# The next tile's loads issued in another order, in a recommender kernel on one core

## What is computed

```
e  = stack of tbl_f[ids[:, f]], f = 0..31        # [1024, 32, 16], called x0
xk = x0
for W in (W0, W1, W2):                            # W: [32, H, 64]
    xk = relu(einsum('bmd,bhd,mhk->bkd', x0, xk, W))
    outs.append(sum of xk over d)                 # 64 numbers per sample and layer
h  = concat(outs, dense_ctx)                      # 208 features
y  = relu(relu(h @ W_top1 + b1) @ W_top2 + b2) @ W_top3
```

## Time and profile before

| | |
|---|---|
| timed runs, median (lowest, highest) | 689.96 us (688.97, 692.24) |
| profiled execution, first to last instruction | 769.5 us |
| granted TensorE clock, mean | 0.918 |
| PE busy | 609.3 us, 79% |
| DVE busy | 577.9 us, 75% |
| POOL busy | 469.8 us, 61% |
| ACT busy | 236.9 us, 31% |
| DMA, all queues | 149.77 MB, mean 195 GB/s |

### The profile page before, as it was taken

The page is one execution under the profiler, slowest core; times in us unless marked ns, Lnnn a source line. Parts: engine busy times, 40 slices in busy tenths (PEclk is TensorE's granted clock), DMA queues, the critical chain, the costliest instruction groups (busy, mean ns, idle before and its releaser), DMA issues.

```text
span 769.5 us, 8172 instructions
## 1 busy us (share of the span) xinstructions
PE 609.3 (79%) x2818; PEld 219.3 (28%) x2818; DVE 577.9 (75%) x292; ACT 236.9 (31%) x440; POOL 469.8 (61%) x362
## 2 busy tenths in 40 slices
PE   0265179949996699939996499996997399999998
PEld 0121023313331134303332133322332133333334
DVE  0003199949994699849995599985995499999994
ACT  0022144206331154306431063425331063325331
POOL 6757447845797168853897258945897248704630
PEclk9978579979998699969999699998999599999999
DMA  5059800699039940699019950499329950399300
GB/s 169 7 154 373 306 1 1 226 356 366 21 124 327 363 153 4 193 393 361 19 41 333 377 214 5 146 342 373 104 56 337 358 215 6 105 376 372 105 1 0
DMA packets 58834, 149.77 MB, mean 195 GB/s; under 512 B 10728, under 2 KB 24048, under 8 KB 58816
## 3 DMA queue, kind: packets, MB, share of 16 engines
q1 hardware_dynamic: 50624, 147.42, 52.2%
q0 software_dynamic: 8192, 2.11, 4.2%
HBM read 145.30 MB, written 4.20 MB: 194 GB/s over the span
## 4 chain that ended last, share of the span: by engine, by line
PE 49%; another core or an unknown queue 16%; DVE 13%; issue 12%; ACT 5%; DMA 3%; POOL 1%; SPq 1%; DVEq 0%; ACTq 0%; POOLq 0%
PE acc L695 42%; DVE zd L509 11%; DMA rolled<-x_scratch 2%; DVE zpart L481 2%; ACT xk_ps L558 2%; PE mlp L743 2%; ACT xk_sb L558 2%; POOL emb L402 1%; PE acc L704 1%; POOL zg L414 1%; ACT relu_ab L564 1%; PE xk_ps L774 1%; PE mlp L735 1%; DMA z2d<-dense_t_in 1%
## 5 line engine op out<-in xcount | busy, mean ns | idle before, releaser
L509 DVE TENSOR_TENSOR zd<-rolled,xk_ps 128x2048 f32<-128x2048 f32 x240 | 533.7, 2278 | 134.6 <-issue 51.4
L695 PE MATMUL acc<-zd,w_sb 128*64 128x512 f32 x1664 | 399.5, 615 | 95.4 <-DVE zd L509 62.2
L414 POOL TENSOR_TENSOR zg<-rolled,xk_sb 128x1024 f32<-128x1024 f32 x96 | 225.8, 2379 | 174.8 <-ACT xk_sb L558 148.3
L402 POOL DMA_INDIRECT emb<-tbl_in,ids_tile x192 | 182.3, 949 | 69.6 <-issue 68.2
L695 PEld LDWEIGHTS acc<-zd,w_sb 128*64 128x64 f32 x1664 | 117.1, 140 | 341.2 <-issue 218.2
L558 ACT ACTIVATE xk_ps<-acc 64x512 f32<-64x512 f32 x128 | 73.0, 570 | 210.1 <-PE acc L695 122.9
L564 ACT ACTIVATE relu_ab<-acc 128x512 f32<-128x512 f32 x48 | 28.7, 597 | 259.5 <-PE acc L695 237.2
L695 PE MATMUL acc<-zg,w_sb 128*64 128x512 f32 x384 | 100.1, 601 | 2.4 <-POOL zg L414 2.4
L695 PE MATMUL acc<-zd,w 128*64 128x512 f32 x256 | 65.1, 636 | 18.0 <-issue 11.2
L402 POOL DMA_INDIRECT emb<-tbl_in,ids_sb x64 | 60.6, 946 | 27.1 <-issue 24.9
L558 ACT ACTIVATE xk_sb<-acc 64x512 f32<-64x512 f32 x128 | 75.7, 591 | 3.1
(11 more groups left out here) (74 smaller groups left out, 149.4 us busy)
## 6 DMA issues: line engine op xcount, KB each, us to landing
rolled<-x_scratch SPq DMA_DIRECT2D x252, 512.0 KB
xk_sb<-x_scratch SPq DMA_DIRECT2D x15, 512.0 KB
x_scratch<-x0t SPq DMA_DIRECT2D x16, 256.0 KB
emb<-tbl_in,ids_tile POOLq DMA_INDIRECT x192
emb<-tbl_in,ids_sb POOLq DMA_INDIRECT x64
w_sb<-w_in SPq DMA_DIRECT2D x2, 512.0 KB
zg<-select_in SPq DMA_DIRECT2D x1, 640.0 KB
wt<-wtop_in SPq DMA_DIRECT2D x1, 512.0 KB
```

The lines of the kernel that those rows point to most:

```text
L402: pool.indirect_dma_start(emb[:, f * DIM:(f + 1) * DIM], None, tables[f], bass.IndirectOffsetOnAxis(index[:, f:f + 1].bitcast(U32), 0)).th ...
L414: nc.gpsimd.tensor_tensor(zg[:, plan_of(t).slot("pool", n), :], rolled[:, j, s * STREAM:(s + 1) * STREAM], xk_sb[:, s, :], ALU.mult).then_ ...
L509: nc.vector.tensor_tensor(zd[:, plan_of(t).slot("dve", n), 0:w, :], rolled[:, j:j + w, s * STREAM:(s + 1) * STREAM], twice(xk_ps[:, s, :], ...
L695: last = nc.tensor.matmul(acc[h * MAPS:(h + 1) * MAPS, s, :], weights, z[:, h * HALF:(h + 1) * HALF], start=(i == 0 and c == 0), stop=(i = ...
```

## The change

The order of the loads becomes: chunks 0 to 15 of x, the base of x, chunks 0 to 3 of y, the base of y, chunks 4 to 15 of y. Counted from 1, the base of x moves from place 1 to place 17, chunks 0 to 3 of x from places 2 to 5 to places 1 to 4, the base of y from place 6 to place 22, chunks 0 to 3 of y from places 7 to 10 to places 18 to 21, and chunks 4 to 15 of x from places 11 to 22 to places 5 to 16. Chunks 4 to 15 of y stay at places 23 to 34. The value that SyncE waits for ahead of each chunk is also put in a register first (`known`, L273).

```diff
@@ -308,8 +308,7 @@
             first = L0CH
 
-            load_order = ([(0, j) for j in range(-1, first)] + [(1, j) for j in range(-1, first)]
-                          + [(0, j) for j in range(first, NCH)] + [(1, j) for j in range(first, NCH)])
+            load_order = [(0, j) for j in (*range(NCH), -1)] + [(1, j) for j in (*range(first), -1, *range(first, NCH))]
@@ -381,7 +380,7 @@
                             load_base(s)
                         else:
 
-                            sp.wait_ge(*freed[(s, j)])
+                            sp.wait_ge(freed[(s, j)][0], known(freed[(s, j)][1]))
                             load_rolled(s, j)
```

## The result

The changed kernel takes 782.06 us (median, 774.9 to 788.06), the kernel before 690.63 beside it. The ratio is 1.129, with a 95% interval of 1.122 to 1.137. That is 91 us or 13% slower; 775 had been forecast. The lowest and the highest run of the changed kernel lie in the range of 744 to 796, but the sum behind the forecast has two errors that nearly cancel each other, and a second trace of the kernel before shows them.

What follows compares the result with a forecast made beforehand. VectorE was taken to set the pace, with TensorE close behind and no load waited for. Seven boundaries at 13.2 us of delay add 92 us to 690, less 7 us gained: 775 us, with an 8-in-10 range of 744 to 796.

Steps and rivals of the forecast that it cites:

- The mechanism: Twice a tile, ScalarE waits to copy a late base; VectorE has two gaps, about 9 and 4 us, at no chunk.
- the step on the base of y: Phase 1 waits for the base of y's copy, 13.2 us later per tile, including 9.5 us for the base of x.
- From phase 1 to the next L nothing changes: From phase 1 to the next tile's first load issue (L), the time stays 48.2 us.
- The wait for chunks 4 to 15 of x: These chunks come 6 places earlier; VectorE and TensorE waited for none, at slower boundaries at most a few us.
- 7 us in all: Gain from earlier chunks, GpSimd's vanished wait and hidden idle time: 1 us a tile, bounds 0 and 15 us.
- Place 22: Base of y's place in the load queue: lands about 35.5 us after the first load's issue, phase 1 at 36.8.
- Place 17: Base of x's place in the load queue: lands 27.5 us after the first load's issue, delaying phase 0 by 9.5 us.
- nearly all of this idle time belongs to the profiled execution alone: Waits without a named releaser, 94.7 us of the 769.5 us span, are nearly all absent from timed runs; 675 us remain.
- grow by less than 85 us: Sign in the profiled span: at six boundaries the new wait lies partly under idle time already there.
- The rival with the hidden wait: Unnamed idle time in timed runs already delays phase 1, hiding the new wait: 685 to 690 us, chance 0.06.
- The best pace: Rival: all loads move at 417 GB/s, so phase 1 is delayed 8.9 us a tile: 745 us, chance 0.12.
- The clock: Rival: TensorE's clock falls during idle time at each boundary, 14 us more: 789, or 796 with slower transfers; chance 0.08.

Runs made afterwards that it cites:

- the run of 811.71 us: Changed kernel's load order with GpSimd's chunks ahead of the others inside each group, timed where the kernel before took 769.42 us: 811.71 us, ratio 1.055.

## Why the prediction was right, and where it was off

- **The mechanism** was right. The two waits stand at ScalarE's copies of the bases and at no chunk, twice a tile. The waits overlap, as the step on the base of y said ("The 9.5 us are part of these 13.2"); the kernels with one base late show it.
- **"From phase 1 to the next L nothing changes"** was wrong. For the changed kernel 48.5 us is right. But in the kernel before that stretch takes 53.6, not 48.2. The 48.2 came from tiles of the first trace in which an unnamed idle time had stood ahead of phase 1, and in such a tile GpSimd's chunks are no longer late. The stretches were read behind a delay, and were taken for those of a kernel without one. The wait for chunks 4 to 15 of x was seen ("at most a few us" at the slower boundaries) but priced at 1 us a tile, and it is 5.1. So I allowed 7 us in all for what the change hides, with a bound of 15, and it is 31.
- **Place 22 "at about L + 35.5"** was too early by 4 us: phase 1 starts at L + 41.0 in the mean, not L + 36.8. The step took the pace of one boundary, 344 GB/s, for all, and 323 is the mean of seven. That is 2.3 us (12.2 MB take 37.8 us). The rest is that more than 12.2 MB had been moved by then, 12.8 in the mean. Place 17 was out by more: the base of x is copied at L + 32.5 in the mean, not from L + 27.5 on, but that lies within the delay of phase 1. The boundary from tile 6 to 7 is also the only one in which GpSimd issues no gathers for a later tile. After the change it has L + 38.8, and the first six have 41.4 in the mean. But the sixth, with its gathers, has 38.5, so gathers alone don't explain it, and why the boundaries differ stays open. The term is 7 x 17.2 = 120 us in place of 92.
- The two errors, +28 and -24 us, nearly cancel. That the sum came so near is luck: with the delay alone put right it would have said 803 us, outside the range.
- **"nearly all of this idle time belongs to the profiled execution alone"** was right in that the timed runs beside it don't have it, and wrong in that no single execution has to be to blame: on another occasion the kernel before took 769.42 us, as the median of seven runs. That the first trace came from such an occasion is inferred from its span. The span without this idle time is also not 675 us. As 10.2 of the 94.7 us are ordinary waits, it is 685, and the second trace has 683.3. The profiled span did grow by less than 85 us, by 3.6, but only because the trace before was of this kind and the one after was not.
- **The rival with the hidden wait** did not decide, but such an occasion shows its mechanism. The ratio of the changed kernel with GpSimd's chunks first is then 1.055 and not 1.125.
- **The best pace** (417 GB/s) came in no boundary. The two paces in the Trainium skill's page "DMA: Bandwidth & Descriptors", section Specifications, of 358 and 435 GB/s, would have given a delay of 10 or 4 us a tile, by the prediction's estimates. The runs show 17, at a pace of 323 GB/s, below both.
- **The clock** fell, to 0.50 of full speed while TensorE was idle, the lower of its two levels. The 256 matmuls of VectorE's products in phases 0 and 1 took 709 ns in the mean, against 598 in the second trace of the kernel before. But hardly any of it came through to VectorE: the stretch from phase 1 to the next L takes 48.5 us, and its shortest length in any trace is 48.2.

The clock's row is the one of the stretch around the copy of the base of x at the last boundary (length, busy times, PEclk, DMA share, GB/s):

```profile
684.20:688.20 4.00, 0.00 (x0) 0.00 (x0) 0.00 (x0) 1.05 (x2) 0.00 (x0) 0.50 1.04 380
```

## What to carry to other kernels

When the transfers are the limit, a load lands by its place in the queue. So put the loads in the order in which the engines come to need them. Here the copy of one base gates a whole phase, and a helper engine begins with the last chunks of a slot. A delay costs only what it exceeds the later waits by that it hides. So measure the stretch behind the place of the delay in a trace that has no delay there. Read the landmarks of all repetitions of a loop, not of the cleanest one alone, and compare a trace's span with the timed runs before using it.

## What was not expected of the hardware

The same kernel, unchanged, had medians of 687.01, 687.27, 689.05 and 690.63 us on four occasions and 769.42 us on a fifth. In the two traces of such occasions, the first of the kernel before and that of the run of 811.71 us, VectorE stands idle for 5 to 20 us at a time, behind the first L in every boundary but the last. The trace names no releaser for it, and the DMA engines move 290 to 390 GB/s meanwhile. Two such stretches, one from each trace (length, busy times of PE, PEld, DVE, ACT and POOL, PEclk, DMA share, GB/s):

```profile
416.60:431.40 14.80, 1.06 (x6) 0.14 (x2) 0.03 (x2) 0.00 (x0) 9.58 (x11) 0.71 0.99 342
420.90:440.40 19.50, 4.19 (x20) 1.15 (x16) 0.04 (x1) 0.01 (x1) 12.31 (x14) 0.68 0.96 290
```

What GpSimd does in them is to issue gathers. Behind the first L the two traces have 14 such waits of 6 us or more, and in 13 of them it issues 4 to 13 gathers. The boundary from tile 6 to 7, which has no gathers, has no such wait in either trace. But the undisturbed traces have the same gathers and no such waits, and no run takes the gathers away. So the cause stays open. On such an occasion the changed kernel with GpSimd's chunks first lost 5.5%, on another 12.5%.
